# Plain float32 score products in the big attention layers of an eight-sublayer transformer kernel

## The reference, cut to what matters

```python
q = x @ Wq;  k = ctx @ Wk;  v = ctx @ Wv
q, k = rope(q, k)                      # layer 0
q, k = rmsnorm(q) * wq, rmsnorm(k) * wk   # layers 1 and 3
scores = einsum('bhqd,bhkd->bhqk', q, k) / sqrt(128) + mask
attn = softmax(scores)
out = einsum('bhqk,bhkd->bhqd', attn, v)
x = x + tanh(gate) * (out @ Wo)
```

## Time and profile before

| | before |
|---|---|
| median of three runs (lowest, highest) | 2618.01 us (2615.47, 2619.14) |
| the profiled execution: its own time, its span | 2616.36 us, 2614.6 us |
| TensorE matmuls (PE), busy | 2382.5 us, 91% |
| TensorE weight loads (PEld) | 2016.6 us, 77% |
| VectorE (DVE) | 1786.3 us, 68% |
| ScalarE (ACT) | 1278.9 us, 49% |
| GpSimd (POOL) | 1512.2 us, 58% |
| granted TensorE clock, mean | 0.967 of full |

### The profile page before, as it was taken

One profiled execution on the slowest core, in us unless ns is written; L12 is line 12 of the kernel. 1 busy time (PEld: TensorE's weight loads), 2 busy tenths in 40 slices (PEclk: granted clock), 3 DMA queues, 4 the chain that ended last, 5 costly groups with the idle time before them and its releaser, 6 DMA issues.

```text
span 2614.6 us, 41410 instructions
## 1 busy us (share of the span) xinstructions
PE 2382.5 (91%) x13005; PEld 2016.6 (77%) x13005; DVE 1786.3 (68%) x3406; ACT 1278.9 (49%) x3698; POOL 1512.2 (58%) x1567
## 2 busy tenths in 40 slices
PE   5899999998889999999887887899689999999977
PEld 4788888886778888888766776776578888888753
DVE  4677777777877777777666676563477777777752
ACT  2555555554246666666534455233245666665421
POOL 5666666665246666666535667423456666666543
PEclk9999999999999999999999999899889999999979
DMA  3234444443224233223310000259513233322344
GB/s 110 80 118 155 141 160 159 151 162 109 71 84 142 97 98 102 93 93 98 109 49 17 1 1 27 81 193 365 175 61 108 91 98 101 101 94 77 116 169 151
DMA packets 191532, 288.12 MB, mean 110 GB/s; under 512 B 15985, under 2 KB 110833, under 8 KB 188378
## 3 DMA queue, kind: packets, MB, share of 16 engines
q1 hardware_dynamic: 175584, 236.34, 27.1%
q0 software_dynamic: 10224, 42.03, 4.6%
q10 hardware_dynamic: 5514, 7.11, 0.9%
HBM read 218.80 MB, written 100.37 MB: 122 GB/s over the span
## 4 chain that ended last, share of the span: by engine, by line
PE 73%; DVE 8%; DMA 6%; POOL 5%; issue 4%; ACT 3%; SPq 0%; POOLq 0%; ACTq 0%; DVEq 0%
PE B_qkv L806 32%; PE B_out L806 19%; PE B_more L883 4%; PE B_s L863 4%; PE B_qT L852 3%; DMA slots_y<-S 3%; PE B_more L806 2%; PE B_s L864 1%; PE B_more L957 1%; DMA out_x<-rows_last 1%; PE B_s L806 1%; DVE xn L1523 1%; DVE X L1650 1%; PE B_qT L806 1%; PE B_more L855 1%
## 5 line engine op out<-in xcount | busy, mean ns | idle before, releaser
L1333 ACT ACTIVATE W<-S,nmx 128x128 f32<-128x128 f32 x768 | 298.1, 395 | 49.9 <-DVE nmx L1625 48.8
L2183 POOL TENSOR_TENSOR S<-S,mask 128x512 f32<-128x512 f32 x184 | 256.6, 1394 | 46.9 <-ACT S L1162 46.9
L1226 ACT ACTIVATE sq<-B_qkv 128x640 f32<-128x640 f32 x127 | 89.7, 706 | 380.1 <-PE B_qkv L806 380.1
L2228 POOL TENSOR_TENSOR pT_l<-W,pT_h 128x512 fp32r<-128x512 f32 x184 | 241.8, 1314 | 32.9 <-ACT pT_h L1162 30.7
L2157 POOL TENSOR_SCALAR rn<-ss 128x5 f32<-128x5 f32 x128 | 25.3, 198 | 371.3 <-DVE ss L1563 371.3
L806 PE MATMUL B_qkv<-ring_h,xnT_h 128*128 128x512 f32 x540 | 216.2, 400 | 11.3 <-DVE spare_l L1474 4.8
L2222 POOL TENSOR_TENSOR W<-W,rden 128x512 f32<-128x512 f32 x192 | 202.1, 1052 | 32.7 <-DVE rden L1630 32.6
L806 PE MATMUL B_qkv<-ring_l,xnT_h 128*128 128x512 f32 x540 | 214.5, 397 | 0.0
L806 PE MATMUL B_out<-ring_h,oT_h 128*128 128x512 f32 x516 | 206.1, 399 | 8.7 <-DVE kT L1615 4.4
L806 PE MATMUL B_qkv<-ring_h,xnT_l 128*128 128x512 f32 x540 | 212.8, 394 | 0.0
L863 PE MATMUL B_s<-kT,qT_h 128*128 128x256 f32 x768 | 191.1, 326 | 17.8 <-DVE xnT_l L1474 15.1
(11 more groups left out here) (514 smaller groups left out, 7730.5 us busy)
## 6 DMA issues: line engine op xcount, KB each, us to landing
raw<-in_pieces SPq DMA_DIRECT2D x270, 256.0 KB, 2.6
between_p<-S SPq DMA_DIRECT2D x184, 256.0 KB, 2.2
W<-between_p SPq DMA_DIRECT2D x184, 256.0 KB, 2.8
slots_x<-in_zero SPq DMA_DIRECT2D x32, 1030.0 KB, 6.0
raw<-in_experts SPq DMA_DIRECT2D x16, 768.0 KB, 6.5
w<-in_experts SPq DMA_DIRECT2D x8, 1024.0 KB, 14.0
slots_y<-S SPq DMA_DIRECT2D x31, 256.0 KB, 6.4
xn<-slots_x ACTq DMA_DIRECT2D x8, 257.5 KB, 5.8
```

The lines of the kernel that those rows point to most:

```text
L1333: t = act.activation(W[:, k, cols(r)], S[:, k, cols(r)], ACT.Exp, bias=nmx[:, k, r:r + 1], accum_out=den[:, k, r:r + 1])
L2183: pool.tensor_tensor(S3, S3, m.unsqueeze(1).to_broadcast([P, R, P]), ALU.add).then_inc(*masked.now((layer, u)))
L2228: pool.tensor_tensor(heads_first(pT[1][:, :]), by_block(W[:, k, :]), heads_first(f32(pT[0][:, :])), ALU.subtract).then_inc(*p_split.now((l ...
```

## The change

The queries are copied once, whole, to a new buffer `q_turned` with two places; the key is copied once to one of the two halves of `kT` (the half alternates from unit to unit). `scores` issues one plain float32 product of 128 columns per head. No low planes are made, the separate low part of the scores is gone, and VectorE adds the mask while it reads the scores from PSUM. The key is always turned into the second half of `B_s`, which the scores no longer use. The mask always has its keys in block order; the exponentials of the units whose probabilities TensorE turns put them back in token order. Several steps also get other places: `exp` moves from 71 to 56, in front of the newest unit's `project` (70); `mask` from 56 to 41; `probs` from 9 of the following iteration to 66; `blocks_p` and `store_p` from 21 to 9.2 and 9.3; `load_p` from 62 to 40; `split_p` from 60 to 51.

```diff
             self.at(i + 1, 50, "turn_q", layer, u)
             self.at(i + 1, 50, "split_k", layer, u)
             self.at(i + 2, 40, "scores", layer, u)
-            self.at(i + 2, 41, "low_scores", layer, u)
-            self.at(i + 2, 56, "mask", layer, u)
-            self.at(i + 2, 71, "exp", layer, u)
-            self.at(i + 3, 9, "probs", layer, u)
+            self.at(i + 2, 41, "mask", layer, u)
+            self.at(i + 2, 56, "exp", layer, u)
+            self.at(i + 2, 66, "probs", layer, u)
             if (layer, u) in TURNED_BY_PE:
                 self.at(i + lag - 2, 46 if u == 0 and (layer, 1) in AHEAD else 30, "turn_p", layer, u)
             else:
-                self.at(i + 3, 21, "blocks_p", layer, u)
-                self.at(i + 3, 21, "store_p", layer, u)
-                self.at(i + 3, 62, "load_p", layer, u)
-                self.at(i + lag - 2, 60, "split_p", layer, u)
+                self.at(i + 3, 9.2, "blocks_p", layer, u)
+                self.at(i + 3, 9.3, "store_p", layer, u)
+                self.at(i + 3, 40, "load_p", layer, u)
+                self.at(i + lag - 2, 51, "split_p", layer, u)
             self.at(i + lag - 1, 20, "times_v", layer, u)
             self.at(i + lag, 0, "attn_out", layer, u, needs=five[3:5],
                     frees=[(n, "attn_out", (layer, u), i + lag) for n in five[3:5]] if last else ())
...
+        with ExitStack() as until_turned:
+            q_turned = until_turned.enter_context(nc.sbuf_tensor("q_turned", [P, 2, HG], F32))
...
                 bank_free("qT")
                 for h in range(R):
                     pe.transpose(B_qT[:, cols(h)], qk[:, cols(h)], ident[:, :])
-                bank, name = key_bank(layer, u)
-                bank_free(name)
-                pe.transpose(bank, qk[:, cols(R)], ident[:, :]).then_inc(*qk_turned.now((layer, u)))
-                read["qT"], read[name] = qT_lo.of((layer, u)), kT_lo.of((layer, u))
+                bank_free("kT")
+                pe.transpose(B_kT[:, 0:P], qk[:, cols(R)], ident[:, :]).then_inc(*qk_turned.now((layer, u)))
+                read["qT"], read["kT"] = qT_hi.of((layer, u)), kT_hi.of((layer, u))
 
             def scores(layer, u):
-                pe.wait_ge(*qT_lo.of((layer, u)))
-                pe.wait_ge(*kT_lo.of((layer, u)))
-                bank_free("sc", "kT")
+                k = unit(layer, u)[3]
+                pe.wait_ge(*qT_hi.of((layer, u)))
+                pe.wait_ge(*kT_hi.of((layer, u)))
+                bank_free("sc")
                 for r in range(R):
-                    pe.matmul(B_s[:, cols(r, 2 * P)], qT[0][:, cols(r)], kT_both[:, :], start=True, stop=False)
-                    t = pe.matmul(B_s[:, cols(2 * r)], qT[1][:, cols(r)], kT[0], start=False, stop=True)
+                    t = pe.matmul(B_sc[:, cols(r)], q_turned[:, k, cols(r)], f32(kT[k]), start=True, stop=True)
                 t.then_inc(*scored.now((layer, u)))
-                read["sc"] = read["kT"] = sc_read.of((layer, u))
+                read["sc"] = sc_read.of((layer, u))
 
...
 
             def turn_q(layer, u):
+                k = unit(layer, u)[3]
                 act.wait_ge(*qk_turned.of((layer, u)))
-                for sem, value in qT_reader:
-                    act.wait_ge(sem, value)
-                copy(qT[0][:, :], B_qT).then_inc(*qT_hi.now((layer, u)))
+                if k in qT_reader:
+                    act.wait_ge(*qT_reader[k])
+                copy(q_turned[:, k, :], B_qT).then_inc(*qT_hi.now((layer, u)))
 
             def split_k(layer, u):
-                kind = KINDS[layer]
+                kind, k = KINDS[layer], unit(layer, u)[3]
                 act.wait_ge(*qk_turned.of((layer, u)))
-                for sem, value in qT_reader:
-                    act.wait_ge(sem, value)
+                if k in qT_reader:
+                    act.wait_ge(*qT_reader[k])
                 if layer == 3 and u == 0:
                     act.wait_ge(*kbd_made2.of(NB - 1))
                 scale = wqk[:, layer // 2:layer // 2 + 1] if kind == "norm" else 1.0
                 if kind == "norm" and u == 0:
                     act.wait_ge(*const.of("wqk"))
-                copy(key_rows(layer, u, kT[0]), key_columns(layer, u), scale).then_inc(*kT_hi.now((layer, u)))
+                copy(block_keys(f32(kT[k])), turned_keys(B_kT[:, 0:P]), scale).then_inc(*kT_hi.now((layer, u)))
 
...
                 oT_reader[:] = [attn_out.of(b)]
 
             def scores(layer, u):
-                qT_reader[:] = [scored.of((layer, u))]
-
-            def low_scores(layer, u):
-
-                k = unit(layer, u)[3]
-                act.wait_ge(*scored.of((layer, u)))
-                if layer == 0 and u == 0:
-                    act.wait_ge(*const.of("mask0"))
-                if layer == 3 and u < 2:
-                    for t in range(TILES2 - 2, TILES2):
-                        act.wait_ge(*y_stored[t % 2].of((2, t)))
-                elif k in S_reader:
-                    act.wait_ge(*S_reader[k])
-                copy(per_head(S[:, k, :]), score_parts[:, :, 1, :], SCALE).then_inc(*low_scored.now((layer, u)))
+                qT_reader[unit(layer, u)[3]] = scored.of((layer, u))
...
@@ -1330,8 +1309,10 @@
                 for token in W_reader.get(k, ()):
                     act.wait_ge(*token)
                 for r in range(R):
-                    t = act.activation(W[:, k, cols(r)], S[:, k, cols(r)], ACT.Exp, bias=nmx[:, k, r:r + 1],
-                                       accum_out=den[:, k, r:r + 1])
+                    src, dst = S[:, k, cols(r)], W[:, k, cols(r)]
+                    if (layer, u) in TURNED_BY_PE:
+                        src, dst = block_keys(src), turned_keys(dst)
+                    t = act.activation(dst, src, ACT.Exp, bias=nmx[:, k, r:r + 1], accum_out=den[:, k, r:r + 1])
                 t.then_inc(*exped.now((layer, u)))
...
                 dve.tensor_copy(ident_r, ident[:, :])
                 dve.tensor_scalar(mask2, mask2u[:, :], -1.0, -HIDE, ALU.add, ALU.mult).then_inc(*mask2_made.now(0))
 
-            def turn_q(layer, u):
-                dve.wait_ge(*qT_hi.of((layer, u)))
-                sub(qT[1][:, :], B_qT, f32(qT[0][:, :])).then_inc(*qT_lo.now((layer, u)))
-
-            def split_k(layer, u):
+            def mask(layer, u):
                 kind, g, b, k, vs = unit(layer, u)
-                bank = key_columns(layer, u)
-                hi, lo = (key_rows(layer, u, m) for m in kT)
-                dve.wait_ge(*kT_hi.of((layer, u)))
-                if kind == "rope":
-                    sub(lo, bank, f32(hi)).then_inc(*kT_lo.now((layer, u)))
-                else:
-                    dve.scalar_tensor_tensor(out=lo, in0=bank, scalar=wqk[:, layer // 2:layer // 2 + 1], in1=f32(hi),
-                                             op0=ALU.mult, op1=ALU.subtract).then_inc(*kT_lo.now((layer, u)))
-
-            def mask(layer, u):
-                k = unit(layer, u)[3]
+                hidden = mask0[:, b, :] if kind == "rope" else mask13[:, :]
+                dve.wait_ge(*scored.of((layer, u)))
+                if layer == 0 and u == 0:
+                    dve.wait_ge(*const.of("mask0"))
+                if layer == 1 and u == 0:
+                    dve.wait_ge(*small["mask13"].of(0))
+                if layer == 3 and u < 2:
+                    for t in range(TILES2 - 2, TILES2):
+                        dve.wait_ge(*y_stored[t % 2].of((2, t)))
+                elif k in S_reader:
+                    dve.wait_ge(*S_reader[k])
+                if (layer, u) not in TURNED_BY_PE:
+                    S_reader[k] = p_stored[k].of((layer, u))
                 S3 = per_head(S[:, k, :])
-                dve.wait_ge(*masked.of((layer, u)))
-                dve.scalar_tensor_tensor(out=S3, in0=score_parts[:, :, 0, :], scalar=SCALE, in1=S3, op0=ALU.mult, op1=ALU.add
-                                         ).then_inc(*sc_read.now((layer, u)))
+                dve.scalar_tensor_tensor(out=S3, in0=per_head(B_sc), scalar=SCALE, in1=hidden.unsqueeze(1).to_broadcast([P, R, P]),
+                                         op0=ALU.mult, op1=ALU.add).then_inc(*sc_read.now((layer, u)))
                 dve.wait_ge(*sc_read.of((layer, u)))
                 dve.tensor_reduce(nmx[:, k, :], S3, AX, ALU.max, negate=True).then_inc(*maxed.now((layer, u)))
...
                                        ).then_inc(*roped.now((layer, u)))
 
-            def low_scores(layer, u):
-                kind, g, b, k, vs = unit(layer, u)
-                S3 = per_head(S[:, k, :])
-                m = mask0[:, b, :] if kind == "rope" else mask13[:, :]
-                if layer == 1 and u == 0:
-                    pool.wait_ge(*small["mask13"].of(0))
-                pool.wait_ge(*low_scored.of((layer, u)))
-                if (layer, u) in TURNED_BY_PE:
-                    S4 = S[:, k, :].rearrange("p (r a j) -> p r a j", r=R, j=BLOCKS)
```

(5 more changed lines are left out.)

28 lines of the change are left out of this document (12 added, 16 removed).

## The result

The changed kernel takes 2623.98 us (median of 20 runs, 2613.57 to 2630.81) where the kernel before takes 2616.47 (20 runs, 2612.68 to 2621.74) beside it. The ratio is 1.0027, with an interval of 1.0017 to 1.0036: a little slower, and just beyond the 0.2% that a measurement of this kernel can tell. The profiled execution spans 2622.1 us after, 2614.6 before.

The account below looks back on a forecast made before the run. The prediction took TensorE's projections, 9.053 us apart, to bound 147 steady periods (1,331 us). Terms 17 + 1 - 11 = +7 us gave 2623.4 us profiled, 2625 for the median; range 2602 to 2647, the forecast's own 2619 to 2638.

Parts of the forecast that it names:

- TensorE's own part: Score products on TensorE: four plain ones take 0.90 us where 0.88 stood, +0.02 us a unit, bounds -0.02 and +0.07.
- The four passes of the Trainium skill: Score products: a count of four array passes for true FP32 would give an estimated +53 ns a head, +41 us in all.
- The moved exponentials: Layers 1 and 3, steady periods: `exp` ahead of the square makes a loop 0.17 us over TensorE's period, +17 us.
- The walk: Link-by-link timing of one layer 1 iteration: the loop through transposes, `pT_h`, exponentials, square and `qk` is 0.15 us too long.
- The signs that I named: Profile after: periods 9.15 to 9.3 us in layers 1 and 3, 9.05 to 9.1 in layer 0; first exponential right behind `pT_l`.
- The toll for waiting transposes: TensorE's transposes in the norm layers: 0.66 us when TensorE waits for them, 0.45 when it reaches them late.
- Starts and crossings: About 32 units where TensorE is not the bound: VectorE's saving worth up to 27 us, half taken at the starts, -11 us.
- I cost these at nothing: The other moved steps (reciprocals, `probs`, `blocks_p`, `load_p`, `store_p`) and dropping `key_bank`: no cost.
- the loop doesn't bind: Rival, layers 1 and 3: periods stay 9.05 to 9.07 us, only the starts' gain stands, 2610 us; chance 0.27.
- VectorE's chain through a weight split: Rival, layers 1 and 3: a 1.38 us split before the mask delays exponentials 0.3 to 0.45 us, 2634 to 2650; chance 0.12.
- Streaming: Rival, score products: loading and streaming don't fully hide each other, +13 us over 192 units, 2637 us; chance 0.07.
- terms cancel: Rival, whole kernel: loop of 0.10 us against starts of -11, within 5 us of before; chance 0.20.

Follow-up runs that it names:

- e10: e5 with each of the four score products issued twice, the second writing the same values; 2723.07 us, ratio 1.0402, period 9.947 us in all three layers.
- e2: The changed kernel with only `split_p` moved, from 51 to 49, ahead of the queries' copy; 2601.24 us, ratio 0.9936 to the kernel before.
- e1: The changed kernel's new arithmetic with all seven moved steps back at their old places; 2588.59 us, ratio 0.9884 to the kernel before.
- e3: The changed arithmetic with the new places in layer 0 only, old places in layers 1 and 3; 2592.49 us, ratio 0.9903 to the kernel before.
- e5: The changed kernel with `exp`, `probs`, `blocks_p` and `store_p` back at old places; `mask`, `load_p`, `split_p` stay new; 2581.06 us, ratio 0.9859 to the kernel before.
- e12: e2 with `exp`, `probs`, `blocks_p`, `store_p` at old places for units 54 to 63 of each layer and 0 to 7 of layer 3; 2585.07 us, ratio 0.9862.
- e9: e5 with `exp` early again at 56 and `probs` left at the next unit's 9; 2686.34 us, ratio 1.0256 to the kernel before.
- e7: e1 with the key turned into the shared bank of the kernel before instead of its own; 2590.72 us, ratio 0.9886 to the kernel before.
- e8: e1 plus one VectorE instruction of 128x512 in each unit that changes no values; 2592.33 us, ratio 0.9897 to the kernel before.
- e6: e1 with only `mask` early, at 41 instead of 56; 2580.85 us, ratio 0.9855 to the kernel before.
- e11: The changed kernel with only `exp` and `probs` back at old places, `blocks_p` and `store_p` staying new; 2948.89 us, ratio 1.1258 to the kernel before.
- e4: The kernel before, with its old products, given the changed kernel's new places of the steps; 2696.07 us, ratio 1.029 to the kernel before.

## Why the prediction came out, point by point

**TensorE's own part: right.** I took +0.02 us a unit; the period of layer 0 is unchanged to 0.001 and e10 gives 0.89 for four products, where I took 0.90 in bounds of 0.86 to 0.95. The term is 0 instead of +1 us. The nearest row by number of columns, the 8-column one, was a good guide; its 0.115 a record is 0.003 too high. The four passes of the Trainium skill come near for one product (an estimated 0.213 us by the count, 0.223 measured), but the +41 us that follow if the old products are counted by their columns too did not come: four records of 256 columns and four of 128 took 0.88 as well.

**The moved exponentials: right, by its own walk.** The walk gave 0.15 us, I took 0.17, and it is 0.135; in the trace the exponentials follow the transposes by 3.64 us (the walk had 3.56), the square follows them by 1.56 (1.53), `qk` the square by 3.11 (3.14). The signs that I named are there: `pT_l` releases the exponentials, the square comes straight behind them, and layer 0 stays at 9.05. The toll for waiting transposes, which I feared might be 0.21, is 0.05. The term is +13 us instead of +17. e2 shows that it is this loop.

**Starts and crossings: the step that failed, twice, with opposite signs.** "If VectorE's 0.83 us (the upper value) came off each, they would save 27 us ... I take half": the arithmetic alone gives 27.5 to 31 us (e1), so the upper value was the right one. And "I cost these at nothing", of the moved steps, with +5 us at most at the end: they cost 35 - 13 = 22 us there (e3, e5, e12). The net of my term was -11. By the spans of the profiled executions that of the runs is -27.5 + 21.6 = -6, and the sum is 0 + 13 - 6 = +7, as measured; by the medians it is -31 + 22 = -9 and the sum +4. So the total was right by luck: two errors of 16 to 20 and 22 us stood against each other, and nothing in the reasoning deserved that. I walked the steady iteration link by link and gave the forty or so units at the edges a few sentences. There I looked for VectorE's time between the exponentials and the sum, 0.7 us a unit. Where I followed the loss in the traces (e5's rows), it is a late piece of weights that reaches the next projection through the exponentials, some 3 us at a place, and 1.5 us more of low granted clock behind it. Nowhere did I think of the clock.

**The rivals.** That the loop doesn't bind is refuted by the period. VectorE's chain through a weight split is refuted for the change, where that split takes 0.68 us, and real in e9, where the long units of layer 1 are 0.9 us over 9.05, more than the 0.3 to 0.45 that I gave it (the transposes at 21 stand in that chain too; the longer split alone makes 9.96 of 9.30). The longer split shows as the earlier trace rows had it: 1.35 us beside GpSimd's 1.04 us over `W`, 0.68 without. Streaming is refuted by e10. That terms cancel is what happened, though not the terms I meant.

**What stays open.** What the 28 to 31 us of the arithmetic are made of: the bank shows no gain (e7, to within some 8 us), one VectorE instruction is 4 us by the medians and 10 by one execution (e8), and some 6 us or more lie behind the last unit, where the versions with the new products in the table take 128 to 131 us to the end of their span and both with the old ones 137 and 139; I haven't followed that part. How much the mask at 41 is worth (e6) is open too, and so is the split of the 22 us at the edges between TensorE's waits and the granted clock behind them. The best versions, e5 and e6, are 1.4% faster than the kernel before.

## What to carry to other kernels

- When a change has two halves (cheaper work and a new order), price each at the edges too, and run each alone. Here a total near nothing hid about -30 and +35, and undoing four steps of the order (e5) made the kernel 1.4% faster than before.
- A step moved ahead in a queue brings along all that it waits for. Ask of each such wait what happens when its source is late once, as a load can be, and not only in the steady iteration.
- Moved steps hold each other up. Against the kernel before, taking back two of the seven gave +12.6% (e11) and taking back three, without the exponentials, +2.6% (e9); the four that belong together gave -1.4% (e5). To undo a move, undo the ones that belong to it.

## What the runs showed that I had not expected

- Plain float32 products of 128 columns run at 0.1116 us a record, two records a product, when eight or sixteen follow each other (e10: +0.893 us for four products). Here, following each other closely doesn't slow them.
- A misplaced wait can cost more than its own length: the block transposes wait 2.75 us (e11), and the period rises by up to 4.3, because the normalisation that they wait for stands in GpSimd's queue behind `rn`, which waits for VectorE's sum, and a weight split.
- The transposes of the change wait a little for `qk` and lose little beside the wait: 0.05 us over the five of them (0.49 against 0.44 to the key's), although such a group shows as 0.66 us in place of 0.60.
- A wait of TensorE at the end of a layer is paid twice: behind 3.21 us without work the granted clock stood at 0.50 for 3.4 us, and the next period was 1.5 us longer than in e5.
- GpSimd's addition of the mask takes 1.59 to 1.78 us beside a subtraction of 128x512 on VectorE, and 1.31 without it (e4); VectorE's subtraction takes 1.35 us beside GpSimd's pass over `W`, and 0.68 without it (e9).
